# A layer norm's inverse square root computed on VectorE with a bit trick and three Newton rounds, in place of Ln and Exp on ScalarE

## What is computed

```
o  = gla_scan(x@Wq, x@Wk, x@Wv, log_sigmoid(x@w1@w2 + b2)/16)   # 4 heads, keys 256, values 512
o  = o * rsqrt(mean(o*o) + 1e-5) * g_norm_w * silu(x@Wg)
x  = layernorm(x + o@Wo)
xr, xk = mixes of x and x shifted by one token (mu_r, mu_k)
x  = layernorm(x + sigmoid(xr@Wr.T) * (square(relu(xk@Wk.T)) @ Wv.T))

def _layernorm(x, axis=-1, eps=1e-5):
    m = jnp.mean(x, axis=axis, keepdims=True)
    v = jnp.var(x, axis=axis, keepdims=True)
    return (x - m) / jnp.sqrt(v + eps)
```

## Time and profile before

| | us |
|---|---|
| median of the 2 runs shown | 2449.84 |
| lowest and highest | 2423.79, 2475.88 |
| the profiled execution's own time | 2425.52 |
| its span, slowest core (core 5) | 2424.0 |
| spans of the 8 cores | 2405.5 to 2424.0 |

### The profile page before, as it was taken

The page is one execution under the profiler, slowest core; times in us unless marked ns, Lnnn a source line. Parts: engine busy times, 40 slices in busy tenths (PEclk is TensorE's granted clock), DMA queues, the critical chain, the costliest instruction groups (busy, mean ns, idle before and its releaser), DMA issues.

```text
span 2424.0 us, 30917 instructions; the slowest of 8 cores (2405.5 to 2424.0 us)
## 1 busy us (share of the span) xinstructions
PE 1835.8 (76%) x11776; PEld 1126.4 (46%) x11776; DVE 1132.7 (47%) x2227; ACT 660.1 (27%) x897; POOL 63.2 (3%) x81
## 2 busy tenths in 40 slices
PE   0477877778877787877886888888888687778775
PEld 0245554445444554445544545545545344444443
DVE  0145443445435454454542333333334367776775
ACT  0222222222223222232222323323323233222221
POOL 0000000000000000000000000000000000000000
PEclk9979887788788798787888989989999799998998
DMA  7410111100111001111038312213312611111111
GB/s 99 68 27 4 24 27 27 27 23 5 27 27 26 22 6 27 27 27 35 1 68 159 105 63 94 105 53 105 105 53 91 135 70 70 70 70 70 65 63 47
DMA packets 70707, 134.25 MB, mean 55 GB/s; under 512 B 3985, under 2 KB 36754, under 8 KB 70562
## 3 DMA queue, kind: packets, MB, share of 16 engines
q0 software_dynamic: 28256, 81.93, 14.6%
q1 hardware_dynamic: 42306, 50.35, 6.0%
HBM read 113.53 MB, written 50.33 MB: 68 GB/s over the span
## 4 chain that ended last, share of the span: by engine, by line
PE 56%; DVE 18%; ACT 9%; DMA 9%; issue 8%; DVEq 0%; ACTq 0%; POOLq 0%; SPq 0%
PE PO L584 10%; PE PBIG L554 8%; PE PBIG L316 6%; PE PBIG L349 5%; PE PO L365 5%; PE PBIG L721 4%; PE PO L472 3%; DVE F L331 3%; PE PO L709 3%; PE PO L479 2%; PE PBIG L454 2%; PE PBIG L421 2%; DVE B L727 1%; DVE F L746 1%; DVE V L323 1%
## 5 line engine op out<-in xcount | busy, mean ns | idle before, releaser
L584 PE MATMUL PO<-arena,O 128*128 128x512 bf16 x1024 | 254.8, 415 | 67.8 <-DVE O L573 57.3
L554 PE MATMUL PBIG<-B,arena 128*128 128x256 bf16 x2048 | 230.9, 274 | 15.7 <-ACT B L537 15.3
L554 PEld LDWEIGHTS PBIG<-B,arena 128*128 128x128 bf16 x2048 | 199.3, 98 | 45.6 <-issue 21.7
L584 PEld LDWEIGHTS PO<-arena,O 128*128 128x128 bf16 x1024 | 106.4, 105 | 212.8 <-issue 113.5
L323 DVE CAST V<-PBIG 128x512 bf16<-128x512 f32 x128 | 86.6, 687 | 173.3 <-PE PBIG L316 170.0
L472 PE MATMUL PO<-B 128*128 128x256 bf16 x512 | 119.0, 321 | 42.5 <-DVE PM L448 42.3
L490 ACT ACTIVATE SQ<-PO 128x1024 bf16<-128x1024 f32 x64 | 65.6, 1024 | 291.5 <-PE PO L479 291.5
L316 PE MATMUL PBIG<-arena,B 128*128 128x512 bf16 x512 | 130.5, 422 | 9.5 <-ACT F L307 9.5
L316 PE MATMUL PBIG<-arena,B1u 128*128 128x512 bf16 x512 | 129.0, 419 | 9.8 <-ACT F L307 9.8
L595 DVE SCALAR_TENSOR_TENSOR F<-PO,X 128x1024 f32<-128x1024 f32 x32 | 39.2, 1224 | 207.4 <-PE PO L584 207.4
L565 DVE TENSOR_SCALAR V<-F,gnw_s 128x256 bf16<-128x256 f32 x256 | 73.4, 350 | 131.5 <-ACT F L561 131.5
(11 more groups left out here) (122 smaller groups left out, 2986.1 us busy)
## 6 DMA issues: line engine op xcount, KB each, us to landing
orms<-O SPq DMA_DIRECT2D x16, 1024.0 KB
X<-x POOLq DMA_DIRECT2D x16, 1024.0 KB, 5.3
O<-orms POOLq DMA_DIRECT2D x16, 1024.0 KB, 8.2
ybuf<-Y SPq DMA_DIRECT2D x16, 1024.0 KB
Y<-ybuf POOLq DMA_DIRECT2D x16, 1024.0 KB, 5.3
out<-X SPq DMA_DIRECT2D x16, 1024.0 KB
X<-x POOLq DMA_DIRECT2D x16, 512.0 KB, 7.7
arena<-wv POOLq DMA_DIRECT2D x1, 4096.0 KB, 29.5
```

The lines of the kernel that those rows point to most:

```text
L554: fns.append(lambda E, m=m, mm=mm, kc=kc, b0=b0: E.matmul(PBIG[:, b0 * 512 + mm * 256:b0 * 512 + (mm + 1) * 256], arena[:, A2_WG + kc * 20 ...
L584: fns.append(lambda E, tb=tb, ng=ng, kc=kc, p=po: E.matmul(p[:, ng * 512:(ng + 1) * 512], ot[:, kc * 256 + tb * 128:kc * 256 + tb * 128 + ...
```

## The change

In `emit_ln_tail`, Ln and Exp on ScalarE go. In their place VectorE adds 1e-5 to the variance (x), converts x's bits, read as int32, to a float, takes 0x5f3759df minus half of that, and converts the result back to int32, whose bits read as f32 are a first guess of 1/sqrt(x). Three rounds of y = y * (1.5 - 0.5 * x * y * y), four instructions each, follow. Each of the 16 is a group of its own that writes `statr`, so each waits on the one before. The negative mean moves to columns 24 and 25 of `statr`, which grows from 20 to 32 columns. The layer norm's last instruction is as before but for the columns that it reads. The norm in `scan_tail` of stage A1 keeps its Ln and Exp.

```diff
-        statr = sb("statr", [128, 20], F32)
+        statr = sb("statr", [128, 32], F32)
...
             S.group("vector", [lambda E: E.tensor_scalar(
-                statr[:, 16:18], statr[:, 4:6], -1.0, None, ALU.mult)], writes=[bSTAT])
-            S.group("scalar", [lambda E: E.activation(statr[:, 12:14], statr[:, 10:12],
-                                                      AF.Ln, bias=EPS)],
-                    writes=[bSTAT])
-            S.group("scalar", [lambda E: E.activation(statr[:, 14:16], statr[:, 12:14],
-                                                      AF.Exp, scale=np.float32(-0.5))],
-                    writes=[bSTAT])
-            fns = [lambda E, tb=tb: E.tensor_scalar(
+                statr[:, 24:26], statr[:, 4:6], -1.0, None, ALU.mult)], writes=[bSTAT])
+            x, fb, y0, ya, tt, yb = (statr[:, 12:14], statr[:, 14:16],
+                                     statr[:, 16:18], statr[:, 18:20],
+                                     statr[:, 20:22], statr[:, 22:24])
+            for fn in [
+                lambda E: E.tensor_scalar(x, statr[:, 10:12], float(EPS), None, ALU.add),
+                lambda E: E.tensor_copy(fb, x.bitcast(I32)),
+                lambda E: E.tensor_scalar(y0, fb, -0.5, MAGICF, ALU.mult, ALU.add),
+                lambda E: E.tensor_copy(ya.bitcast(I32), y0),
+            ]:
+                S.group("vector", [fn], writes=[bSTAT])
+            cur = ya
+            for it in range(3):
+                nxt = yb if cur is ya else ya
+                for fn in [
+                    lambda E, c=cur: E.tensor_tensor(tt, c, c, ALU.mult),
+                    lambda E: E.tensor_tensor(tt, tt, x, ALU.mult),
+                    lambda E: E.tensor_scalar(tt, tt, -0.5, 1.5, ALU.mult, ALU.add),
+                    lambda E, c=cur, n=nxt: E.tensor_tensor(n, c, tt, ALU.mult),
+                ]:
+                    S.group("vector", [fn], writes=[bSTAT])
+                cur = nxt
+            rcol = statr[:, 18:20] if cur is ya else statr[:, 22:24]
+            fns = [lambda E, tb=tb, rc=rcol: E.tensor_scalar(
                 dstt[:, tb * 1024:(tb + 1) * 1024], srct[:, tb * 1024:(tb + 1) * 1024],
-                statr[:, 16 + tb:17 + tb], statr[:, 14 + tb:15 + tb],
+                statr[:, 24 + tb:25 + tb], rc[:, tb:tb + 1],
                 ALU.add, ALU.mult) for tb in range(2)]
```

More of the change, by code:

```diff
@@ L10 @@
 ALU = mybir.AluOpType
+I32 = mybir.dt.int32
+MAGICF = float(0x5f3759df)
 L = 4096
```

## The result

| us | before | after |
|---|---|---|
| median of all runs (6 and 7) | 2424.09 | 2454.56 |
| lowest | 2419.58 | 2450.44 |
| span of the profiled execution | 2424.0 | 2454.1 |
| spans of the 8 cores | 2405.5 to 2424.0 | 2427.7 to 2454.1 |

The changed kernel is slower: the ratio is 1.0124, 95% interval 1.011 to 1.0138, some 30 us.

A forecast was written before the change was run, and what follows sets the result against it. The layer norm's tail was taken to set TensorE's time in A2 already. A2's 16.4 us plus 2.4 at the end, B and hand-over 0, gave 18.8 on 2425.5: 2444 us, 8-in-10 range 2428 to 2468.

The forecast's parts named there:

- The chain of line 622 to the silu: Stage A2: last statistic to next tile's first silu, 5.12 us; TensorE's third quarter of gate matmuls (line 554) starts 0.12 behind.
- 0.27 us for each added instruction: Each tail on VectorE: 0.27 us start to start for all 16, conversions included; line 630 comes 2.38 us later.
- 15 x 1.09 = 16.4 us in A2: Stage A2: 2.38 us more on VectorE less 1.29 of reload leaves 1.09 in each of 15 tiles.
- The clock taken at 0: A2 tiles: change in TensorE's granted clock priced at 0, with ends of -4 and +10 us.
- B at 0: Stage B: 2.38 us more per tail goes into line 727's pauses of 2.89 us or more, costing 0.
- the hand-over at 0: Between A2 and B: TensorE waits for a weight transfer until 1909.96 anyway, so the later line 630 costs 0.
- the end at +2.4: Last tail: nothing stands beside it and only the store follows, so its delay adds 2.4 us.
- Rival 1: A2 does not pay: silu not releasing the third quarter, or loads giving back more; 2424 to 2430 us, chance 0.12.
- Rival 3: Table loads stay before every first silu, A2 paying 2.38 instead of 1.09 per tile; 2464 us, chance 0.04.
- Rival 2: B's cover breaks at line 727 from 0.32 us a step; 2474 us at 0.35, chance 0.05.
- The drain of 1.4 us: ScalarE table switches: a skill page adds some 1380 ns per load; by it A2 would be -4 us instead of +16.4.

The follow-up runs named there:

- experiment 6: A2's silus written to two halves of Ss instead of F1, each its own buffer: changed kernel 1.0063, kernel before 1.0019, both against the kernel before.

## Why the prediction was wrong in size, and where it was right

- **The chain of line 622 to the silu, the third quarter locked 0.12 behind it.** Right: the silu's wait is what the changed kernel loses by. The same 0.11 to 0.12 stands in the tiles of both kernels, A2's tail alone gives 1.0116, and two rounds instead of three give 1.41 us a tile back.
- **0.27 us for each added instruction, the conversions like the rest.** Right: 169 ns for each conversion, and 4.59 us for the 17 steps in 80 of the 112 tiles with the load on SyncE's queue. In the changed kernel the mean is 4.75.
- **15 x 1.09 = 16.4 us in A2.** This is the step that failed. The mechanism was right and the term too small: 25.6 us on the median core. Line 630 was carried over at 1.53 us to a place 2.4 us later, without a look at what other engines do there. In the trace of before, GpSimd's issue of O's load began just 0.2 us behind line 630, held back until X's load had landed. That the two didn't meet was an accident of timing, and the later line meets it: 0.21 us in line 648 and 0.06 of the 0.16 in the steps. The prediction says that no DMA is moved; but the work was moved past one. The other 0.10 in the steps is the late step that stays without GpSimd's issue, and 0.26 a tile lies outside the pause, about half of it by the clock.
- **The clock taken at 0, with +10 us as its end.** By the estimate above it was 0.15 x 15 = 2 us, and 0.26 x 15 = 4 at most, within that spread. The reasoning behind it, a new pause too short to matter, held at 1.8 us and would have failed at 3.1. The time at 1.2 GHz does not simply grow with the pause (experiment 6), which nothing in the prediction foresaw, so that it came out near 0 was partly luck.
- **B at 0, the hand-over at 0, the end at +2.4.** Right: 1.0011 for the tail in B alone, 30.8 against 28.3 us behind the last relu, the median pause from 3.25 to 0.8.
- **Rival 1, the silu isn't what releases the third quarter:** excluded by the TensorE rows. **Rival 3, the reloads stay:** excluded by one load each. **Rival 2** needed 0.32 us a step; 4.75 / 17 is 0.28. The drain of 1.4 us that the prediction weighed under rival 1 is in no row, not even with the loads brought back.
- **2444 us and the range.** 2454.6 lies in the range of 2428 to 2468, but the change of +30 us is over half as large again as the +18.8. That the range held it is partly luck: its upper end stood on the reloads staying and on dear conversions, and neither came. And the sentence that two per cent is about what can be told from no change was too coarse: the runs tell 1.24% from nothing, to within 0.14%. A forecast of +18.8 us was one of a clear loss, and should have been given so.

## What to carry to other kernels

Before moving work off an engine, find who waits behind it and add up that chain on the new engine with its semaphore steps, not the busy time: 62 table loads, 80 us of ScalarE, were removed and the kernel lost 30 us. When a long instruction shifts by 2 us, look at what GpSimd and the queues do at its new place, since they are not drawn in its own chain. And if TensorE has one long pause in a loop, look at that first: filling it gained 76 us, while a saving of 0.3 us a tile beside it was swallowed by the clock.

## What the runs showed of the hardware that I had not expected

- VectorE's 128x1024 f32 scale, 1.53 us for two, took up to 2.21 us beside a GpSimd DMA issue, and the issue up to 1.71 us instead of 1.18. The stretched instruction always ended 0.48 to 0.50 us behind the issue. With the load on another queue: 1.53 to 1.54 in every tile.
- The granted clock can settle: of the tiles of 34.93 us of work and waits, 104 of 112 were of the slowest kind, 37.55 us at the median. A kernel with a little more waiting had a better mean.
- A pause of 3.1 us ahead of a matmul quarter, besides the one of 3.76, went with 3.5 us more of each tile at 1.2 GHz than one of 0.28 us; one of 1.8 us with 0.3.
- A table load behind 6.3 us in which ScalarE had nothing to do cost its 1283 ns and nothing that the rows show beyond it.
